# Another order for the guests of the last image: each chunk's score four places behind its variance

## The chip, the cores and the metric

The kernel runs on one core of a Trainium2 chip. The metric is device time in microseconds; smaller is better. The core's engines run side by side and are held together by semaphores alone: TensorE (PE) multiplies matrices and writes PSUM, VectorE (DVE) and ScalarE (ACT) compute element by element, GpSimd (POOL) multiplies the band of the attention and issues the stores of the output, SyncE (SP) issues the loads.

## What is computed

One layer of a vision transformer over a batch of four images. The patches of each image are embedded and a class token goes in front: 3137 tokens of 128 features. Then

```python
h = tok(x, tok_W, tok_b, tok_cls)
h = h + attn(layernorm(h), Wq, Wk, Wv, Wo, bias_table)      # 8 heads of 16
h = h + ffn(layernorm(h), attn_w, attn_b, gate_w, gate_b, w1, b1, w2, b2)

def ffn(x, ...):                       # x: the second layernorm's result
    aw = softmax(x @ attn_w + attn_b, axis=1)            # a score for each token
    pooled = sum(x * aw, axis=1)
    gates = softmax(pooled @ gate_w + gate_b)
    idx = top_k(gates, 2)                                # two of 8 experts per image
    g = gates * mask(idx); g = g / (sum(g) + 1e-9)
    h = gelu(x @ w1 + b1)                                # 128 -> 512
    eo = gelu(h @ w2 + b2)                               # 512 -> 128
    return sum over the two experts of eo * g
```

The gate of an image needs the scores of all its tokens, and these need the second layernorm of all its tokens.

## The kernel before

Features lie on the 128 partitions, tokens along the free dimension. An image has 8 chunks (`CH`) of W = 393 tokens. The kernel has three stages: embedding, first layernorm and projections; attention over 32 pairs of image and head; and the experts.

**Guests.** What lies between attention and experts is cut into 33 small pieces for each image, called guests, which stand as single steps inside another stage's stream. For a chunk c they are:

- Y: TensorE multiplies the chunk's attention output by Wo; VectorE adds it to `h_all` (line 1100).
- M: TensorE takes the mean over the features with the matrix `mean_w`; VectorE subtracts it (1104) and squares the difference into `sq2[c % 2]` (1106).
- V: TensorE takes the mean of the squares, the variance; VectorE adds epsilon into `root` (1108) and computes the reciprocal square root with `rstd`: a first guess from integer bits (1125), three Newton rounds of three instructions (1130, 1132, 1135 or 1137), and the multiplication of the chunk by the result (1140). That last instruction raises `s_ln2`.
- S: TensorE multiplies the normalized chunk by `pool_wr`; VectorE adds the bias (1112): the score.
- G, one for the image: the logits of the gate.

The guests of the first three images stand in the attention of the following image. Those of the last image have no attention left to stand in: they stand beside the steps of the expert loop.

**The expert loop.** 64 units (4 images, 8 chunks, 2 experts) and one step more. In step U TensorE does in this order: eight matmul instructions of the first layer of unit U (line 773), eight of the second layer of unit U - 1 (781), and, where `LATE` has a guest for the step, that guest (`visit`, 757). ScalarE does four Gelus of the hidden layer (916) and one of the output (923). VectorE accumulates the output of the unit before into `h_all` (1210) and then takes the guest's result out of PSUM (`receive`). Each engine works through its own list in order, and a wait holds back all that is behind it.

**The order.** `LATE` gives step 3 + i the guest number i of the last image, for i from 0 to 31; which guest that is comes from `guest_list`, the order of `guest_plan()`, which is laid out for the attention of the other images. Written out with the steps it begins Y0 3, M0 4, V0 5, S0 6, Y1 7, M1 8, Y2 9, V1 10, S1 11, M2 12, V2 13, S2 14, Y3 15, and ends Y7 31, M7 32, V7 33, S7 34. For each of the eight chunks S stands one step behind V. The maximum of the scores follows in step 36 (`pool_max`, VectorE), their exponential (`pool_exp`, ScalarE) in step 36 too, the pooling in 37, the gate guest in 39 and the choice of experts in 40.

**What a guest waits for** (`visit`, lines 735 to 757): Y for its chunk of attention output, which SyncE loads into `att[c % 4]`; M for its Y; V for the squares of its M (`s_sq2`); S for its chunk's normalization (`s_ln2`). All use the same PSUM bank (`LATE_PS`), so guest k also waits until k guests have been taken out by VectorE (`s_guest`). For V the first instruction (1108) counts as the taking, not the end of the chain.

**SyncE.** `load_attention(b, c)` (583 to 591) loads the chunks 0 to 3 of the last image at the end of the attention; the chunks 4 to 7 use the same four buffers and wait until Y of chunk c - 4 has been taken. `load_experts(b)` (593 to 602) loads the weights of two experts of an image. At the end of SyncE's list stand: the weights of the second image, the chunks 4 to 7, and the weights of the third and of the fourth image, each behind a step of the expert loop.

The lines that the change touches are the list of orders, `guest`, which turns a number into image, kind and chunk, and `guest_number`, which does the reverse.

Of the kernel before, what the change touches and what calls it, by code (L numbers as in the profile page):

```python
# [20 lines left out]
CH = 8  # L21
# [69 lines left out]
def guest_plan():  # L91

    seen = {"Y": 0, "M": 0, "V": 0, "S": 0}
    plan = []
    for p in range(1, 2 * HEADS):
        y_here = False
        for pos in GUEST_POS:
            if pos == GUEST_POS[2]:
                kinds = [("V", "M")]
            else:  # L100
                kinds = [("S", "V"), ("M", "Y"), ("Y", None)]
            for kind, after in kinds:
                c = seen[kind]
                if c < CH and (after is None or c < seen[after]) and not (kind == "Y" and y_here):
                    seen[kind] += 1
                    y_here = y_here or kind == "Y"
                    plan.append((kind, c, p, pos))
                    break
    assert len(plan) == 4 * CH and plan[-1][2] <= 13
    return plan + [("G", 0, 15, GUEST_POS[0])]  # L110


def fast_order(B, KT):

    NBH = B * HEADS
    PASS = 4 * KT
    units = [(n, kt, 4 * side + c) for n in range(NBH) for side in range(2) for kt in range(KT) for c in range(4)]
    plan = guest_plan()
    places = [(2 * HEADS * (b + 1) + p) * PASS + pos for b in range(B - 1) for kind, c, p, pos in plan]
    busy = {q // PASS for q in places} | {2 * HEADS * (b + 1) + p for b in range(B - 1) for p in (13, 14, 15)}  # L120
    wanted = [q * PASS + pos for q in range(1, 2 * NBH) for pos in ((33, 53) if q in busy else (28, 46, 64, 82))]

    def plain(u):

        n, kt, c = units[u]
        lo = kt * P - REACH
        return kt < KT - 1 and max(lo, c * (-(-((KT - 1) * P + 65) // CH)), 0) >= min(lo + BAND, (c + 1) * (-(-((KT - 1) * P + 65) // CH)))

    groups, guest_at, d_at, u = [], {}, {}, 0
    while u < len(units):  # L130
        size = GMAX
        if len(guest_at) < len(places) and u >= places[len(guest_at)]:
            guest_at[len(groups)] = len(guest_at)
            size = GMAX - 1
        elif len(d_at) < len(wanted) and u >= wanted[len(d_at)] and u + 2 < len(units) and plain(u + 2):
            d_at[len(groups)] = len(d_at)
        groups.append(list(range(u, min(u + size, len(units)))))
        u += size
    assert len(guest_at) == len(places)
    batches = [list(range(m, m + 4)) for m in range(0, len(units), 4)]  # L140
    return units, groups, batches, guest_at, d_at


def build(nc, B, S, d):
# [27 lines left out]
    with top:  # L172
# [34 lines left out]
        with ctx:  # L207
# [196 lines left out]
            GUESTS = 4 * CH + 1  # L404
            D_STEPS = 6
            EW = 16 * 8
            NU = 2 * CH
            GATE_OPS = 15
            guest_list = [(kind, c) for kind, c, p, pos in guest_plan()]
            chunk_pass = {c: p for kind, c, p, pos in guest_plan() if kind == "Y"}  # L410

            def guest(k):

                return (k // GUESTS,) + guest_list[k % GUESTS]

            def guest_number(b, kind, c):

                return b * GUESTS + guest_list.index((kind, c))

            def expert_unit(U):  # L420

# [73 lines left out]
            def _(sp):  # L495
# [87 lines left out]
                def load_attention(b, c):  # L583

                    if c >= 4:
                        sp.wait_ge(s_guest, guest_number(b, "Y", c - 4) + 1)
                    elif b > 0:
                        sp.wait_ge(s_guest, guest_number(b - 1, "Y", c + 4) + 1)
                    head = CH * 32 * W
                    src = bass.AP(att_rows, b * (HEADS * head) + c * 32 * W, [[head, HEADS], [W, HD], [1, W]])  # L590
                    sp.dma_start(att[:, c % 4], src).then_inc(s_att[c % 4], 16)
# [56 lines left out]
            def _(pe):  # L648
# [85 lines left out]
                def visit(k, bank):  # L734

                    b, kind, c = guest(k)
                    x = slice(c * W, (c + 1) * W)
                    if kind == "Y":
                        if k == 0:
                            pe.wait_ge(s_w3, 16 * 5)  # L740
                        pe.wait_ge(s_att[c % 4], 16 * (b * CH // 4 + c // 4 + 1))
                        weight, moving, n = wo[:], att[:, c % 4], W
                    elif kind == "M":
                        pe.wait_ge(s_guest, guest_number(b, "Y", c) + 1)
                        weight, moving, n = mean_w[:], h_all[:, b, x], W
                    elif kind == "V":
                        pe.wait_ge(s_sq2, b * CH + c + 1)
                        weight, moving, n = mean_w[:], sq2[:, c % 2], W
                    elif kind == "S":
                        pe.wait_ge(s_ln2, b * CH + c + 1)  # L750
                        weight, moving, n = pool_wr[:], x2[b][:, x], W
                    else:
                        pe.wait_ge(s_pooled, b + 1)
                        weight, moving, n = pooled[:], gate_w[:], E
                    if k > 0:
                        pe.wait_ge(s_guest, k)
                    nc.tensor.matmul(ps[:, bank, 0:n], weight, moving, start=True, stop=True).then_inc(s_guest_mm, 1)  # L757
# [231 lines left out]
            def _(dve):  # L989
# [103 lines left out]
                def receive(k, bank):  # L1093

                    b, kind, c = guest(k)
                    x = slice(c * W, (c + 1) * W)
                    came = ps[:, bank, 0:W]
                    dve.wait_ge(s_guest_mm, k + 1)
                    if kind == "Y":
                        nc.vector.tensor_tensor(h_all[:, b, x], h_all[:, b, x], came, ALU.add).then_inc(s_guest, 1)  # L1100
                    elif kind == "M":
                        if c == 0 and 0 < b < B - 1:
                            dve.wait_ge(s_ln2_out[b - 1], 16)
                        nc.vector.tensor_tensor(x2[b][:, x], h_all[:, b, x], came, ALU.subtract).then_inc(s_guest, 1)
                        dve.wait_ge(s_guest, k + 1)
                        nc.vector.tensor_tensor(sq2[:, c % 2], x2[b][:, x], x2[b][:, x], ALU.mult).then_inc(s_sq2, 1)
                    elif kind == "V":
                        nc.vector.tensor_scalar(root[:, 0], came, EPS, None, ALU.add).then_inc(s_guest, 1)
                        dve.wait_ge(s_guest, k + 1)
                        rstd(b, c, x)  # L1110
                    elif kind == "S":
                        nc.vector.tensor_scalar(sc2[b][:, x], came, pool_b[:, 0:1], None, ALU.add).then_inc(s_guest, 1)
                    else:
                        nc.vector.tensor_tensor(gt[:, b, 0], ps[:, bank, 0:E], gate_b[:], ALU.add).then_inc(s_guest, 1)
                        dve.wait_ge(s_guest, k + 1)
                        g0 = b * GATE_OPS
                        nc.vector.reduce_max(st[:, b, 5:6], gt[:, b, 0], AX_X).then_inc(s_gates, 1)
                        dve.wait_ge(s_gates, g0 + 1)
                        nc.vector.tensor_scalar(st[:, b, 6:7], st[:, b, 5:6], -1.0, None, ALU.mult).then_inc(s_lg, 1)
# [1017 lines left out]
```

## Time and profile before

| | |
|---|---|
| median of three runs | 2872.43 us (2869.24 to 2874.86) |
| the profiled execution | 2869.71 us, of which 2868.0 are the span |
| mean granted clock of TensorE | 0.986 |
| busy share of the span | TensorE 88%, ScalarE 88%, VectorE 56%, GpSimd 30% |
| attention | from 205 to 2453 us (first and last exponential of scores) |
| expert loop | from 2455 us to the end, the guests of the last image from 2474 us |

The span is the time from the first to the last instruction of the profiled execution. A timeline row gives the start in us from the span's start, the duration in us, the engine, the line of the kernel, the operation, what it writes and reads, the shape, and how many instructions are merged; in brackets stands the engine's idle time just before and what ended it. Names of tiles are those of the memory, which several tiles share: `halves` is `att`, `qk_sq` is `sq2`, `shared` is the normalized last image and its scores, `qa` and `ka` are the hidden layer and the output of the experts. A matmul's `x8` are four products of 128x128 by 128x393 in two instructions each; PEld is the loading of weights, which runs beside the matmuls.

### The profile page before, as it was taken

The page shows a single profiled execution, that of the slowest core. Times are in us where ns is not written, and L with a number is a line of the kernel's source. Part 1 is how long each engine was busy: PE and PEld are TensorE (multiplying, and loading weights), DVE is VectorE, ACT ScalarE, POOL GpSimd, SP SyncE. Part 2 cuts the span into 40 slices and gives each one's busy share as a digit, 9 for nine tenths or more (in the row PEclk, how much of TensorE's full clock was granted, in tenths as well). Part 3 has the DMA queues.
Part 4 walks back from the last instruction along what each step waited for, and adds up shares of the span by engine and source line. Part 5 has one row for each costly group of instructions (what it writes and reads, how often), then busy time and mean ns, then how long its engine had stood idle before and what let it go on. Part 6 is the DMA issues. An engine that isn't in the chain of part 4 may idle for free.

```text
span 2868.0 us, 123840 instructions
## 1 busy us (share of the span) xinstructions
PE 2534.1 (88%) x55860; PEld 1252.9 (44%) x55860; DVE 1616.4 (56%) x2542; ACT 2524.5 (88%) x2733; POOL 873.1 (30%) x1424
## 2 busy tenths in 40 slices
PE   7988888888888888988889898888989888999897
PEld 3444444444444444444444444444444444555454
DVE  5754777776756556555565565565655654443310
ACT  5669999999999999999999999999999999544453
POOL 2113443333333333333333333333333333100000
PEclk9989999999999999999999999999999999999999
DMA  5540101100101110011111000111110011210010
GB/s 145 172 163 12 38 32 33 32 29 29 41 29 35 32 32 29 29 51 43 30 36 33 29 29 29 51 40 35 32 32 29 29 52 46 91 35 14 14 35 19
DMA packets 65911, 125.43 MB, mean 44 GB/s; under 512 B 10034, under 2 KB 55180, under 8 KB 63892
## 3 DMA queue, kind: packets, MB, share of 16 engines
q1 hardware_dynamic: 63324, 110.93, 12.4%
q8 instruction: 446, 7.31, 1.1%
q0 software_dynamic: 2048, 6.43, 0.6%
q14 instruction: 93, 0.76, 0.1%
HBM read 67.30 MB, written 51.30 MB: 41 GB/s over the span
## 4 chain that ended last, share of the span: by engine, by line
ACT 46%; PE 25%; issue 18%; DVE 6%; DMA 3%; POOL 0%; SPq 0%; ACTq 0%; DVEq 0%; POOLq 0%
ACT shared L897 45%; PE ps L812 6%; PE ps L773 5%; PE ps L781 5%; PE ps L730 3%; PE ps L757 2%; PE ps L727 2%; DMA k_halves<-halves 1%; DVE root L1087 1%; PE ps L669 1%; DVE std L1019 1%; DVE root L1080 1%; DVE root L1078 1%; DVE root L1132 0%; DVE root L1130 0%
## 5 line engine op out<-in xcount | busy, mean ns | idle before, releaser
L897 ACT ACTIVATE shared<-ps 128x1179 f32<-128x1179 f32 (+1 forms) x2167 | 2205.8, 1181 | 34.1 <-PE ps L730 18.3
L812 PE MATMUL ps<-shared,va 64*32 64x393 f32 x25600 | 1565.4, 500 | 1.3 <-issue 0.9
L980 POOL TENSOR_TENSOR shared<-shared,e_all 128x310 f32<-128x310 f32 (+19 forms) x1344 | 814.9, 623 | 1441.5 <-ACT shared L897 1434.5
L730 PE MATMUL ps<-qa,ka 48*32 48x393 f16 (+1 forms) x15200 | 733.8, 319 | 138.3 <-ACT shared L897 122.2
L727 PE MATMUL ps<-qa,ka 51*32 51x393 f16 (+8 forms) x13184 | 658.9, 313 | 122.4 <-ACT shared L897 114.0
L812 PEld LDWEIGHTS ps<-shared,va 64*32 64x32 f32 x25600 | 617.3, 139 | 31.9 <-issue 5.2
L730 PEld LDWEIGHTS ps<-qa,ka 48*32 48x32 f16 x15200 | 242.6, 90 | 603.5 <-ACT shared L897 575.1
L727 PEld LDWEIGHTS ps<-qa,ka 51*32 51x32 f16 x13184 | 218.5, 89 | 641.4 <-ACT shared L897 621.8
L1057 DVE COPY xc<-ps 128x393 f32<-128x393 f32 x64 | 36.4, 569 | 533.2 <-PE ps L812 533.2
L1087 DVE SCALAR_TENSOR_TENSOR root<-root 128x393 f32<-128x393 f32 x486 | 319.6, 658 | 16.7
L916 ACT ACTIVATE qa<-ps,b 128x393 f32<-128x393 f32 x256 | 136.6, 586 | 111.6 <-PE ps L773 111.5
L1210 DVE SCALAR_TENSOR_TENSOR h_all<-ka,gsc,h_all 128x393 f32<-128x393 f32 x64 | 40.2, 628 | 263.5 <-ACT ka L923 263.5
L1078 DVE TENSOR_SCALAR root<-ps 128x393 f32<-128x393 f32 x162 | 91.8, 567 | 141.1 <-PE ps L727 71.3
L1065 DVE RECIPROCAL sq<-sq 128x393 f32<-128x393 f32 x64 | 167.4, 2615 | 2.2
L985 POOL DMA_DIRECT2D out<-h_all x32 | 18.0, 563 | 380.0 <-DVE h_all L1210 380.0
L923 ACT ACTIVATE ka<-ps,b 128x393 f32<-128x393 f32 x64 | 37.8, 591 | 98.3 <-PE ps L781 98.3
L1082 DVE SCALAR_TENSOR_TENSOR root<-root 128x393 f32<-128x393 f32 x162 | 109.5, 676 | 5.5
L1091 DVE SCALAR_TENSOR_TENSOR shared<-root 128x393 f32<-128x393 f32 x162 | 109.2, 674 | 5.5
L1019 DVE RECIPROCAL std<-std 128x393 f32<-128x393 f32 x32 | 83.7, 2615 | 34.0 <-ACT std L844 34.0
L1080 DVE SCALAR_TENSOR_TENSOR root<-root,ps 128x393 f32<-128x393 f32 x162 | 91.7, 566 | 5.5
L773 PE MATMUL ps<-shared,e_all 128*128 128x393 f32 x256 | 93.1, 508 | 0.0
L781 PE MATMUL ps<-qa,v_sb 128*128 128x393 f32 x256 | 89.9, 493 | 0.0
(149 smaller groups left out, 1629.7 us busy)
## 6 DMA issues: line engine op xcount, KB each, us to landing
qa<-q_halves SPq DMA_DIRECT2D x64, 196.5 KB
ka<-k_halves SPq DMA_DIRECT2D x64, 196.5 KB
att_rows<-std SPq DMA_DIRECT2D x64, 196.5 KB, 4.0
v_rows<-v_sb SPq DMA_DIRECT2D x4, 1600.0 KB, 6.9
va<-v_rows SPq DMA_DIRECT2D x32, 200.0 KB, 15.9
ln_rows<-ln SPq DMA_DIRECT2D x32, 196.5 KB, 5.6
q_halves<-halves SPq DMA_DIRECT2D x32, 196.5 KB, 3.1
k_halves<-halves SPq DMA_DIRECT2D x32, 196.5 KB, 4.3
```

Source lines behind the costliest of these rows:

```text
L727: last = nc.tensor.matmul(out[x:y, 0:cut], ka[r:r + 51, par, k0 + x:k0 + y], qa[r:r + 51, par, q0:q0 + cut], start=True, stop=True, tile_p ...
L730: last = nc.tensor.matmul(out[x:y, cut:W], ka[r:r + 48, par, k0 + x:k0 + y], qa[r:r + 48, par, q0 + cut:q0 + W], start=True, stop=True, ti ...
L773: last = nc.tensor.matmul(ps[:, HID_PS + sl, 0:W], w1[b % 2][:, e, sl * P:(sl + 1) * P], ln2[b][:, c * W:(c + 1) * W], start=True, stop=True)
L781: last = nc.tensor.matmul(ps[:, EO_PS + U % 2, 0:W], w2[b % 2][:, e, sl], hid[:, (U - 1) % 2, sl], start=(sl == 0), stop=(sl == HS - 1))
L812: last = nc.tensor.matmul(ps[quad:quad + 32, O_PS + half, 0:W], va[r:r + 64, par, :, kt], pr[r:r + 64, g % SLOTS_PR, j], start=(kt == 0), ...
L897: nc.scalar.activation(pr[:, g % SLOTS_PR, 0:m], ps[:, b0:b0 + m, 0:W], ACT.Exp, scale=-1.0 / (LOG2E * LIFT * LIFT)).then_inc(s_exp, 1)
L916: last = nc.scalar.activation(hid[:, U % 2, sl], ps[:, HID_PS + sl, 0:W], ACT.Gelu, bias=b1[:, 2 * (b % 2) + e, sl:sl + 1])
L980: nc.gpsimd.tensor_tensor(p, p, e_all[0:keys, n % HEADS, t:t + z - a], ALU.mult).then_inc(s_biased, 1)
L1065: nc.vector.reciprocal(inv[:, side], inv[:, side]).then_inc(s_inv, 1)
L1078: nc.vector.tensor_scalar(whole, score, EXP2_OFFSET, ROUND, ALU.add, ALU.add).then_inc(s_d_step, 1)
L1080: nc.vector.scalar_tensor_tensor(x, whole, ROUND, score, ALU.subtract, ALU.subtract).then_inc(s_d_read, 1)
L1087: nc.vector.scalar_tensor_tensor(p, p, EXP2[3 - i], x, ALU.add, ALU.mult).then_inc(s_d_step, 1)
```

## The change

A function `late_order` builds another order for the 33 guests of the last image. It walks over CH + 3 rounds; in round s stand the transform of chunk s, the mean of chunk s - 1, the variance of s - 2 and the score of s - 3, each where there is such a chunk, and G at the end. `guest` and `guest_number` use it for the last image and the old list for the others. The steps of the loop at which guests stand, and the engines' code for each kind, are the same. The unused `chunk_pass` goes.

```diff
+def late_order():
+
+    steps = []
+    for s in range(CH + 3):
+        for kind, lag in (("Y", 0), ("M", 1), ("V", 2), ("S", 3)):
+            if 0 <= s - lag < CH:
+                steps.append((kind, s - lag))
+    return steps + [("G", 0)]
...
             guest_list = [(kind, c) for kind, c, p, pos in guest_plan()]
-            chunk_pass = {c: p for kind, c, p, pos in guest_plan() if kind == "Y"}
+
+            late_list = late_order()
 
             def guest(k):
 
-                return (k // GUESTS,) + guest_list[k % GUESTS]
+                return (k // GUESTS,) + (guest_list if k // GUESTS < B - 1 else late_list)[k % GUESTS]
 
             def guest_number(b, kind, c):
 
-                return b * GUESTS + guest_list.index((kind, c))
+                return b * GUESTS + (guest_list if b < B - 1 else late_list).index((kind, c))
```

The new order is Y0, Y1, M0, Y2, M1, V0, Y3, M2, V1, S0, Y4, M3, V2, S1, and so on in fours, with Y7, M6, V5, S4, M7, V6, S5, V7, S6, S7 at the end.

## Rows read from the trace of the kernel before

**Rows 1.** The page: the span; busy us, share and instructions of each engine.

```profile
span 2868.0 us, 123840 instructions
...
PE 2534.1 (88%) x55860; PEld 1252.9 (44%) x55860; DVE 1616.4 (56%) x2542; ACT 2524.5 (88%) x2733; POOL 873.1 (30%) x1424
```

**Rows 2.** Waits of TensorE from 2453 us on: us in total, times, longest.

```profile
PE ps L757 <- DVE shared L1140: 18.5, 8, 2.4
PE ps L773 <- ACT qa L916: 5.0, 1, 5.0
```

**Rows 3.** Timeline of TensorE: Y0, V0, S0 [idle before it], Y1.

```profile
2473.93 0.82 PE L757 MATMUL ps<-halves,wo 128*128 128x393 f32 x2
...
2485.82 0.82 PE L757 MATMUL ps<-qk_sq,mean_w 128*128 128x393 f32 x2
...
2494.23 0.93 PE L757 MATMUL ps<-shared,pool_wr 128*128 128x393 f32 x2 [2.30 <-DVE shared L1140]
...
2500.28 0.82 PE L757 MATMUL ps<-halves,wo 128*128 128x393 f32 x2
```

**Rows 4.** Timeline of TensorE: V1, S1, the group behind, the next guest.

```profile
2518.12 0.82 PE L757 MATMUL ps<-qk_sq,mean_w 128*128 128x393 f32 x2
...
2526.54 1.00 PE L757 MATMUL ps<-shared,pool_wr 128*128 128x393 f32 x2 [2.31 <-DVE shared L1140]
2527.33 4.47 PE L773 MATMUL ps<-ln,v_sb 128*128 128x393 f32 x8
...
2534.28 0.82 PE L757 MATMUL ps<-h_all,mean_w 128*128 128x393 f32 x2
```

**Rows 5.** Timeline of ScalarE in one step of the expert loop.

```profile
2506.43 0.59 ACT L923 ACTIVATE ka<-ps,b 128x393 f32<-128x393 f32 x1 [1.58 <-PE ps L781]
2508.47 1.07 ACT L916 ACTIVATE qa<-ps,b 128x393 f32<-128x393 f32 x2 [1.45 <-PE ps L773]
2509.73 1.07 ACT L916 ACTIVATE qa<-ps,b 128x393 f32<-128x393 f32 x2 [0.19 <-PE ps L773]
```

**Rows 6.** Timeline of VectorE: accumulation, V0 taken, its chain's end, accumulation.

```profile
2486.64 0.63 DVE L1210 SCALAR_TENSOR_TENSOR h_all<-ka,gsc,h_all 128x393 f32<-128x393 f32 x1 [4.24 <-ACT ka L923]
2487.19 0.56 DVE L1108 TENSOR_SCALAR root<-ps 128x393 f32<-128x393 f32 x1
...
2493.61 0.57 DVE L1140 SCALAR_TENSOR_TENSOR shared<-root,shared 128x393 f32<-128x393 f32 x1
2494.09 0.62 DVE L1210 SCALAR_TENSOR_TENSOR h_all<-ka,gsc,h_all 128x393 f32<-128x393 f32 x1
```

**Rows 7.** Windows behind S0, S1: busy us by engine, clock, DMA share, GB/s.

```profile
2494.20:2502.20 8.00, 7.97 (x24) 4.66 (x25) 2.23 (x4) 2.73 (x5) 0.54 (x1) 1.00 0.07 25
2526.50:2534.50 8.00, 7.96 (x19) 4.49 (x20) 1.15 (x2) 2.15 (x5) 0.00 (x0) 0.79 0.00 0
```

**Rows 8.** Timeline of TensorE: the group 32 steps behind the first guest.

```profile
2691.61 2.80 PE L773 MATMUL ps<-shared,v_sb 128*128 128x393 f32 x8
```

**Rows 9.** Timeline of SyncE's queue: loads of attention chunks and ln rows.

```profile
2462.74 2.72 SPq L591 DMA_DIRECT2D halves<-att_rows  x4
2465.56 0.94 SPq L607 DMA_DIRECT2D shared<-ln_rows  x2
...
2478.01 1.10 SPq L591 DMA_DIRECT2D halves<-att_rows  x1
```

**Rows 10.** Windows while the loads run, columns as in group 7.

```profile
2470.00:2480.00 10.00, 10.00 (x32) 5.77 (x31) 1.20 (x3) 4.86 (x9) 0.71 (x1) 1.00 1.03 379
2480.00:2484.00 4.00, 4.00 (x14) 2.31 (x13) 1.67 (x3) 2.29 (x5) 0.55 (x1) 1.00 0.59 181
```

**Rows 11.** Timeline of TensorE: the group behind the wait on ScalarE.

```profile
2707.33 5.00 PE L773 MATMUL ps<-shared,v_sb 128*128 128x393 f32 x8 [4.99 <-ACT qa L916]
```

**Rows 12.** Windows without a stall, columns as in group 7.

```profile
2455.20:2491.80 36.60, 36.60 (x114) 20.62 (x110) 13.91 (x23) 17.92 (x33) 1.26 (x2) 1.00 0.49 162
2712.20:2844.70 132.50, 132.50 (x404) 76.22 (x403) 19.73 (x47) 70.94 (x129) 7.05 (x13) 1.00 0.08 27
```

## The prediction

> **What bounds the kernel now.** I read the page first: TensorE and ScalarE are each busy for 88% of the span [rows 1], an average over three different stages, so it prices nothing. The change reaches only the guests of the last image, the small matmuls that stand between the steps of the expert loop, from about 2474 us on. So I asked second what TensorE waited for from the loop's start to the end of the kernel: 18.5 us in eight waits on line 1140, the last instruction of the normalization on VectorE, and one of 5.0 us on ScalarE; there is nothing else [rows 2]. The timeline of TensorE shows the form. A step of the loop with a guest takes 5.95 us: from 2500.28 to 2518.12 there are three of them, 17.84 us, so 5.947 each [rows 3, 4]. Its matmuls stand back to back, thus TensorE sets the pace, and ScalarE idles 1.58 + 1.45 + 0.19 = 3.2 us in each [rows 5]. The exception is the score guest S, which stands one place behind the variance guest V of the same chunk: V0 at 2485.82, S0 not one step later, at 2491.77, but at 2494.23, after 2.30 us idle [rows 3].
>
> VectorE shows why. V's matmul starts at 2485.82; the accumulation of the step goes first (2486.64), line 1108 takes V's result at 2487.19, and the chain ends with line 1140, at 2493.61 + 0.57 = 2494.18 [rows 6], 8.36 us behind V. S reads what that line writes, and TensorE works in order, so all expert matmuls behind S stand still.
>
> The granted clock adds a second loss. Behind S0 the clock stays at 1.00; behind S1 the same 2.31 us of idle time is followed by a stretch at 0.79, in which eight matmuls take 4.47 us rather than 2.80 [rows 4, 7]: part of it at the lower of TensorE's two levels (1.2 against 2.4 GHz). Of the eight stalls, those of chunks 0, 2, 4 and 6 look like the first, those of 1, 3, 5 and 7 like the second: windows of 8 us behind each show 1.00 four times and 0.79 four times, of which one of either kind stands there.
>
> **What a stall costs.** Measured from the start of V to the start of the guest behind S, two steps, which need 2 x 5.947 = 11.89 us. Short kind: 2500.28 - 2485.82 = 14.46, so 2.57 us. Long kind: 2534.28 - 2518.12 = 16.16, so 4.27 us, 1.70 of them the clock's. Four of each: 4 x (2.57 + 4.27) = 27.4 us. A second way that doesn't need the pairs: from the first guest (2473.93) to the start of the group that stands 32 steps behind it (2691.61, [rows 8]) are 217.68 us; 32 steps of 5.947 are 190.3; the difference is 27.4 us.
>
> **What the change does.** It removes no instruction and adds none: the same 32 guests stand at the same steps, 3 to 34, and only their order differs; the maximum, the exponential, the pooling and the gate guest stay at steps 36 to 40. Written out, the variances now stand at steps 8, 11, 15, 19, 23, 27, 30 and 32, and the scores at 12, 16, 20, 24, 28, 31, 33 and 34. So the distance is 4, 5, 5, 5, 5, 4, 3 and 2 steps: four only at the start, and two for the last chunk. Two suffice: S7's turn comes 11.89 us behind V7, and the chain is through after 8.36, with 3.5 us in hand. All eight stalls go, with the clock falls behind them: gain 27.4 us.
>
> **What is late next.** Each guest also waits until the guest before it has been taken out of the one PSUM bank. Now something other than its own score stands behind every variance. That guest is taken only when VectorE is through with the chain, and the guest after it waits for that. From the rows: the chain is through at +8.36, the accumulation at 2494.09 + 0.62 = +8.89, taking a result costs some 0.56 more, as at line 1108 [rows 6], so about +9.5; the matmul that needs the bank has its turn at +11.89. Slack 2.4 us: no stall, price 0, and if the slack weren't there, each us over it would cost 8 us in all. The other distances (transform Y to mean M at least 2, M to V at least 3) are longer than or equal to those of before, where no such pair stalled. VectorE's work per guest is unchanged. ScalarE's wait for an accumulation reaches back more than one step, and the accumulation that the chain delays ends at +8.89 in the old order as well; ScalarE keeps its 3.2 us of idle time. Price 0.
>
> **The moved loads.** The transforms Y1, Y2 and Y3 move from steps 7, 9 and 15 to 4, 6 and 9, and their chunks of the attention output are among the four that SyncE issued from 2462.74 on, ahead of two loads of ln rows at 2465.56 [rows 9] and of the experts' weights. Y1 is the tight one: it now has the turn of 2479.87, 5.95 us behind the first guest. From 2470 to 2480 the DMA engines are full, and by 2484 the queue is nearly empty [rows 10]. The chunks were issued first, some 15 us ahead, and Y0's chunk, of the same group, was there at 2473.93 without a wait; I take price 0. The other end: the chunk comes as the last of all, at 2484, which costs 4.1 us and, with a clock fall, 5.8, and leaves 21.6 us of the gain. The Trainium skill ("DMA: Bandwidth & Descriptors", section "Two DMAs through the same engine are not ordered") says that nothing orders transfers across the 16 DMA engines, so being issued first promises nothing about landing first; by that rule the gain could be 21.6 us in place of 27.4. No row here gives the landing of these chunks.
> The loads of chunks 4 to 7 wait on SyncE for Y0 to Y3. The first was issued at 2478.01 [rows 9], when SyncE was through with the weights, and is needed at step 13, that is at 2473.93 + 10 x 5.947 = 2533; the others are asked for at steps 4, 6 and 9 and needed at 17, 21 and 25, at least 13 steps or 77 us later. Queued behind them on SyncE are the weights of the third image, which wait for a step (17) that doesn't move in the order; they are needed at step 32. Price 0.
>
> **What stays.** The 5.0 us wait on ScalarE behind the last score [rows 2], with matmuls of 5.00 instead of 2.80 us behind it [rows 11], lies at a fixed step and comes 27 us earlier. Its clock fall costs 2.2 us and could come out somewhat larger or smaller: plus or minus 2 us.
>
> **Sum.** The profiled execution took 2869.7 us, a span of 2868.0 and 1.7 around it; less 27.4 this is 2842.3. It lies 2.7 us under the median of the three runs, 2872.43. The forecast is for a median: 2872.4 - 27.4 = **2845.0 us**.
>
> **The rivals.**
> - *The clock falls stay.* If the half-rate stretches have another cause than the stalls, 4 x 1.70 = 6.8 us remain: 2851.8. For it: four equal stalls had none, so the stall alone doesn't decide. Against it: outside of stalls the clock is at 1.00 over 36.6 and over 132.5 us of unbroken matmuls [rows 12]. Chance 4%.
> - *Y1's chunk is late*: 2872.4 - 21.6 = 2850.8. Chance 3%.
> - *Two or three steps are not enough for the last chunks*: if VectorE began the chains of V6 and V7 late, S6 and S7 would stall as now, 2.57 + 4.27: 2851.8. Against it the 3.5 us of slack. Chance 3%.
> - *The change doesn't do what it says.* A wait of the same length takes the stall's place, at the second guest behind each V, because the bank is taken later than I derive: 2872.4. Against it the 2.4 us of slack, eight times in the same form. Chance 3%.
> - *Slower.* The pauses are what keeps TensorE at its upper level, and 190 us without any bring it down for part of the time. Each us of work at 1.2 GHz costs one more. Up to 27.4 of the 190.3 us (14%) at the lower level the kernel still gains, beyond that it loses; with 20% it is 2845.0 + 38 = 2883. Against it stand the 132.5 us at 1.00 at the end of this very loop [rows 12]. Chance 2%.
>
> **How the numbers follow.** The forecast has 85%. A measurement of this kernel can tell about 0.2%, 5.7 us, from no change; the forecast is 1.0% down, and the first three rivals 0.7%. So faster 95%, same 3%, slower 2%. The range: the three runs of before spread over 2869.2 to 2874.9, 3 us to each side, and the term at the ScalarE wait adds 2: 2840 to 2850. It leaves out all rivals, 15%, of which two begin just above it.
>
> **What would show it.** In the profile after: no wait of TensorE on line 1140 in the loop; 32 steps of 5.95 us between the first guest and the group behind the last, 190 us rather than 218; the granted clock at 1.00 over them; a score's matmul starting right behind the expert matmuls while VectorE has been through for several us; the ScalarE wait of 5 us as before; no wait of TensorE before the second Y. I would be wrong if idle time appears on TensorE two steps behind a variance, if matmuls of 4.4 us per eight stand without a stall ahead of them, or if the stretches before 2474 us differ by more than a few us from one run to the next.

## The result and the profile after

The changed kernel takes 2843.11 us (median of four runs, 2842.16 to 2845.30) against 2871.71 us beside it (2869.24 to 2874.86): a ratio of 0.9901, 95% interval 0.9884 to 0.9918, so 28.6 us or 1.0% faster. The forecast was 2845.0 in a range of 2840 to 2850. The profiled execution took 2842.38 us with a span of 2840.7; against the 2869.71 and 2868.0 of before that is 27.3 us.

Lines behind the new function have moved by 11: line 757 is now 768, 773 is 784, 781 is 792, 916 is 927, 1108 is 1119, 1140 is 1151, 1210 is 1221.

The page's busy line of after, which answers to the one in [rows 1]: the same number of instructions on each engine, and TensorE's busy time 12.7 us shorter, though nothing was taken out. Of these, 8.8 us lie in the guests' stretch (199.12 against 190.30 in the two windows below); 6.8 of them are the matmuls that ran at the lower clock, as an experiment below shows.

```profile
PE 2521.4 (89%) x55860; PEld 1249.2 (44%) x55860; DVE 1614.3 (57%) x2542; ACT 2523.4 (89%) x2733; POOL 872.5 (31%) x1424
```

The waits of TensorE from 2453 us on, which answer to [rows 2] (what waited, for what: us in total, times, longest). The eight waits on the end of the chain are not there; the one on ScalarE is, unchanged.

```profile
PE ps L784 <- ACT qa L927: 5.0, 1, 5.0
```

The timeline of TensorE in the loop, which answers to [rows 3, 8, 11]: Y0, Y1, V0, the guest behind it (Y3), the one behind that (M2), S0, the group 32 steps behind the first guest, and the group behind the wait on ScalarE.

```profile
2473.40 0.82 PE L768 MATMUL ps<-halves,wo 128*128 128x393 f32 x2
...
2479.35 0.82 PE L768 MATMUL ps<-halves,wo 128*128 128x393 f32 x2
...
2503.14 0.82 PE L768 MATMUL ps<-qk_sq,mean_w 128*128 128x393 f32 x2
...
2509.08 0.82 PE L768 MATMUL ps<-halves,wo 128*128 128x393 f32 x2
...
2515.03 0.82 PE L768 MATMUL ps<-h_all,mean_w 128*128 128x393 f32 x2
...
2526.92 0.82 PE L768 MATMUL ps<-shared,pool_wr 128*128 128x393 f32 x2
...
2663.69 2.80 PE L784 MATMUL ps<-shared,v_sb 128*128 128x393 f32 x8
...
2679.41 5.15 PE L784 MATMUL ps<-shared,v_sb 128*128 128x393 f32 x8 [4.99 <-ACT qa L927]
```

No guest has idle time ahead of it. From the first guest to the group behind the last are 2663.69 - 2473.40 = 190.29 us, 5.947 a step; before it was 217.68. S0 starts 23.8 us behind V0, when its chain has been through for 15.

VectorE over the same variance, which answers to [rows 6]: accumulation, V0 taken, the end of the chain, the next accumulation, and the guest behind V (Y3) taken.

```profile
2503.96 0.63 DVE L1221 SCALAR_TENSOR_TENSOR h_all<-ka,gsc,h_all 128x393 f32<-128x393 f32 x1 [4.24 <-ACT ka L934]
2504.50 0.56 DVE L1119 TENSOR_SCALAR root<-ps 128x393 f32<-128x393 f32 x1
...
2510.93 0.57 DVE L1151 SCALAR_TENSOR_TENSOR shared<-root,shared 128x393 f32<-128x393 f32 x1
2511.42 0.62 DVE L1221 SCALAR_TENSOR_TENSOR h_all<-ka,gsc,h_all 128x393 f32<-128x393 f32 x1
2511.95 0.56 DVE L1111 TENSOR_TENSOR h_all<-h_all,ps 128x393 f32<-128x393 f32 x1
```

The chain is as long as before, through 8.36 us behind V (2510.93 + 0.57 - 2503.14). The guest behind V is taken by 2511.95 + 0.56 = 2512.51, and the matmul that needs its bank has its turn at 2515.03: 2.5 us in hand.

The guests' 32 steps as one window in the trace of before and in that of after (columns as in group 7; the clock is the third number from the end):

```profile
2474.00:2691.60 217.60, 199.12 (x577) 111.60 (x576) 88.80 (x160) 87.31 (x160) 9.16 (x16) 0.97 0.11 36
```

```profile
2473.40:2663.70 190.30, 190.30 (x578) 109.23 (x577) 88.08 (x160) 87.15 (x160) 9.14 (x16) 1.00 0.12 40
```

TensorE idled 18.5 us of the 217.6 and is now busy without a gap; VectorE and ScalarE did the same work in both.

### The profile page after: what moved, and what is told of

Same layout as the page of the kernel before. It is cut to its first block, busy times and chain, and to the rows that moved or that the text cites. A ratio compares the mean times of both kernels' runs of the same rounds, so it can differ in the third digit from the quotient of the medians.

```text
span 2840.7 us, 123840 instructions
## 1 busy us (share of the span) xinstructions
PE 2521.4 (89%) x55860; PEld 1249.2 (44%) x55860; DVE 1614.3 (57%) x2542; ACT 2523.4 (89%) x2733; POOL 872.5 (31%) x1424
## 4 chain that ended last, share of the span: by engine, by line
ACT 47%; PE 27%; issue 18%; DVE 4%; DMA 3%; SPq 0%; POOL 0%; ACTq 0%; DVEq 0%; POOLq 0%
ACT shared L908 46%; PE ps L784 6%; PE ps L792 6%; PE ps L823 6%; PE ps L741 3%; PE ps L768 3%; PE ps L738 2%; DMA k_halves<-halves 2%; DVE root L1098 1%; DVE std L1030 1%; DVE root L1091 1%; DVE root L1089 1%; PE ps L680 1%; PE ps L674 0%; PE ps L695 0%
## 5 line engine op out<-in xcount | busy, mean ns | idle before, releaser
L741 PE MATMUL ps<-qa,ka 48*32 48x393 f16 (+2 forms) x15200 | 732.9, 319 | 139.4 <-ACT shared L908 122.9
L792 PE MATMUL ps<-qa,e_all 128*128 128x393 f32 x256 | 89.7, 493 | 0.0
```

The costliest lines, as they stand in the source:

```text
L741: last = nc.tensor.matmul(out[x:y, cut:W], ka[r:r + 48, par, k0 + x:k0 + y], qa[r:r + 48, par, q0 + cut:q0 + W], start=True, stop=True, ti ...
L792: last = nc.tensor.matmul(ps[:, EO_PS + U % 2, 0:W], w2[b % 2][:, e, sl], hid[:, (U - 1) % 2, sl], start=(sl == 0), stop=(sl == HS - 1))
```

## The experiments

The theory: TensorE waited, in order, for the chain of the same chunk; that cost 2.30 us of idle time eight times, and part of these pauses brought a fall of the clock. The rivals: that the distances of Y, M and V or the earlier loads brought something; that four places are needed; that the clock falls have another cause; that a wait behind the variance is close by.

All kernels were profiled. The third column is the stretch from the first guest to the group behind the last, read as above, which holds every step that the change touches; the last is its mean granted clock.

| kernel | median us (of before beside it) | 32 steps, us | clock |
|---|---|---|---|
| before | 2871.71 | 217.68 | 0.97 |
| after | 2843.11 (2871.71) | 190.29 | 1.00 |
| score directly behind its variance | 2872.97 (2872.54) | 217.54 | 0.97 |
| old order, score one place later | 2846.37 (2872.54) | 192.91 | 1.00 |
| old order, two rounds | 2852.61 (2872.54) | 196.43 | 1.00 |
| old order, four rounds | 2899.87 (2871.22) | 241.40 | 0.92 |
| old order, pauses filled | 2864.46 (2872.54) | 210.88 | 1.00 |
| new order, four rounds | 2847.46 (2871.22) | 190.29 | 1.00 |
| new order, five rounds | 2854.78 (2871.22) | 200.77 | 1.00 |

### The new order with each score directly behind its variance

```diff
-        for kind, lag in (("Y", 0), ("M", 1), ("V", 2), ("S", 3)):
+        for kind, lag in (("Y", 0), ("M", 1), ("V", 2), ("S", 2)):
```

Expected: 

> The new order with one thing undone: the score of chunk s - 2 is placed in the same round as its variance, so that every S again stands one step behind its own V, while Y, M and V stay apart as in the changed kernel. Theory (S directly behind V is all that the old order cost): the eight waits on the last instruction of the chain come back with 2.3 us each, a step pair of 14.5 us without and 16.2 us with a clock fall, so the time is that of after, 2843.1, plus 8 x 2.57 = 20.6 and 1.7 for each fall: 2863.7 with none, 2870.5 with four, 2877 with eight. Rival (the earlier loads, or the distances of Y, M and V, brought the gain): 2843 to 2850 and no such waits. How often the clock falls is open; the theory says only that it falls behind stalls.

Measured: 2872.97 us, ratio 1.0003 (0.9988 to 1.0018), 2.5 us above what was expected with four clock falls: all of the gain is gone. The waits of TensorE and its timeline at V2, S2, the group behind and the next guest:

```profile
PE ps L768 <- DVE shared L1151: 18.5, 8, 2.4
```

```profile
2567.33 0.82 PE L768 MATMUL ps<-qk_sq,mean_w 128*128 128x393 f32 x2
...
2575.74 1.17 PE L768 MATMUL ps<-shared,pool_wr 128*128 128x393 f32 x2 [2.30 <-DVE shared L1151]
2576.70 4.30 PE L784 MATMUL ps<-shared,e_all 128*128 128x393 f32 x8
...
2583.48 0.82 PE L768 MATMUL ps<-halves,wo 128*128 128x393 f32 x2
```

The same eight waits with the same 18.5 us as in [rows 2], and again the clock fell behind four of the eight: 2583.48 - 2567.33 = 16.15 us is the long kind. They are other ones than before: windows of 8 us behind each show 0.79 or 0.80 for chunks 2, 3, 5 and 7. Y, M and V follow one another as in the changed kernel, from Y3 on one step later because S0 stands ahead of it, and Y1 and Y2 need their chunks as early. The stretch is that of before to 0.14 us. So the distance between V and S is the whole effect, and the other moves bring and cost nothing.

### The old order with the scores one place later

```diff
+    steps = [(kind, c) for kind, c, p, pos in guest_plan()]
+    for c in range(CH - 1):
+        i = steps.index(("S", c))
+        steps[i], steps[i + 1] = steps[i + 1], steps[i]
```

(This stands in `late_order` in place of the four rounds, so it acts on the last image alone; `steps` starts as the old list.)

Expected: 

> The old order with the smallest step away from it: the scores of chunks 0 to 6 change places with the guest behind them, so they stand two steps behind their variance; the last chunk's score stays one behind. Theory (two places are enough, since the chain is through 8.4 us behind V and the turn of S comes at 11.9): seven of eight stalls go, one of 2.57 or 4.27 us stays, 2871.7 - 27.4 + 2.6 to 4.3 = 2846.9 to 2848.6, and the only wait of TensorE on the chain is at the last score. Rival (four places are what it takes): stalls remain at all scores, the time is above 2855.

Measured: 2846.37 us, ratio 0.9912 (0.9889 to 0.9935), half a us below the expected 2846.9 to 2848.6. TensorE's wait on the chain, and its timeline at V0 and S0:

```profile
PE ps L767 <- DVE shared L1150: 2.4, 1, 2.4
```

```profile
2484.21 0.82 PE L767 MATMUL ps<-qk_sq,mean_w 128*128 128x393 f32 x2
...
2496.10 0.82 PE L767 MATMUL ps<-shared,pool_wr 128*128 128x393 f32 x2
```

S0 starts 11.89 us behind V0 without idle time; the one wait on the chain that is left is that of the last chunk, whose score wasn't moved, and it is of the short kind: 192.91 - 190.29 = 2.62 us. For the seven scores that were moved, two places do all that the new order does.

### The old order with a shorter and with a longer chain

```diff
-                    r0 = (b * CH + c) * 9
+                    rounds = 3 if b < B - 1 else 2
+                    r0 = (b * CH + c) * 9 if b < B - 1 else b * CH * 9 + c * 3 * rounds
...
-                    for i in range(3):
+                    for i in range(rounds):
...
-                        if i < 2:
+                        if i < rounds - 1:
```

(The other kernel has 4 in place of the 2. With two rounds the root is less exact; that kernel leaves work out.)

Expected with two rounds: 

> The old order with two rounds of the root iteration in place of three for the last image: three instructions of VectorE fewer in each chain (the root is less exact; that part of the work is left out), 3 x 0.603 = 1.81 us. Theory (TensorE waits for the length of this chain): each stall shrinks from 2.30 to 0.5 us of idle time, 8 x 1.81 = 14.5 us go, and with them the clock falls (6.8) as the pauses are too short for one: 2871.7 - 14.5 - 6.8 = 2850.4. If the falls stay for all their shorter pauses: 2857.2. Rival (the wait has another cause, such as the bank): 2871.7.

Expected with four: 

> The old order with a fourth round of the root iteration for the last image: three instructions of VectorE more in each chain, 1.81 us. Theory: the idle time ahead of each score grows from 2.30 to 4.1 us, 8 x 1.81 = 14.5 us, 2887 with as many clock falls as before; with a fall behind each of the eight longer pauses up to 4 x 1.7 = 6.8 more, 2894. Rival (the chain is hidden elsewhere): 2872.5.

Measured with two: 2852.61 us, ratio 0.9930 (0.9904 to 0.9957). TensorE at V1, S1, the group behind, the next guest:

```profile
2522.05 0.82 PE L757 MATMUL ps<-qk_sq,mean_w 128*128 128x393 f32 x2
...
2528.65 0.93 PE L757 MATMUL ps<-shared,pool_wr 128*128 128x393 f32 x2 [0.49 <-DVE shared L1141]
2529.41 2.80 PE L773 MATMUL ps<-ln,v_sb 128*128 128x393 f32 x8
...
2534.70 0.82 PE L757 MATMUL ps<-h_all,mean_w 128*128 128x393 f32 x2
```

Idle time 2.31 became 0.49: the 1.81 us of three instructions, one for one. The group behind takes 2.80 us, and no fall is left in the stretch: 217.68 - 196.43 = 21.25 us, where 14.5 + 6.8 = 21.3 was expected. (The median lies 2.2 us above the expected 2850.4; this excess is not in the stretch, see the last section.)

Measured with four: 2899.87 us, ratio 1.0090 (1.0068 to 1.0112). Here the expectation (2887 to 2894) missed. The same places:

```profile
PE ps L757 <- DVE shared L1141: 32.9, 8, 4.2
```

```profile
2530.15 0.82 PE L757 MATMUL ps<-qk_sq,mean_w 128*128 128x393 f32 x2
...
2540.37 1.68 PE L757 MATMUL ps<-shared,pool_wr 128*128 128x393 f32 x2 [4.11 <-DVE shared L1141]
2541.84 5.02 PE L773 MATMUL ps<-ln,v_sb 128*128 128x393 f32 x8
...
2549.34 0.82 PE L757 MATMUL ps<-h_all,mean_w 128*128 128x393 f32 x2
```

The wait grew by 1.81 us as expected (32.9 - 18.5 = 14.4). What was mis-sized is the clock. All eight pauses are followed by slow matmuls, and some of the falls cost more than the 1.7 us that was assumed for each. Two steps without a loss take 11.89 us, the pause adds 4.11 and, as with the short kind of before, 0.27 more: 16.27. The pairs took 17.8 to 19.2, here 2549.34 - 2530.15 = 19.19, so 1.5 to 2.9 us of clock loss for each, 16.1 in all against 6.8 in the old order. The stretch is thus 241.40 - 217.68 = 23.7 us longer. The median is 28.6 above that of before beside it; in the profiled execution the loop also began later (first guest at 2482.46), of which more below.

### The pauses filled with matmuls that nobody reads

```diff
                     elif kind == "S":
+                        if b == B - 1:
+                            for _ in range(3):
+                                nc.tensor.matmul(ps[:, LATE_PS + 1, 0:W], mean_w[:], ln[:, 0:W], start=True, stop=True)
                         pe.wait_ge(s_ln2, b * CH + c + 1)
```

Expected: 

> The old order, and ahead of each score's wait TensorE computes three products of 128x128 by 128x393 whose result nobody reads, 6 instructions of 0.33 us, 1.98 us, in what was idle time. The wait itself stays, and its end is set by VectorE as before. Theory (the clock falls come from the pauses): with 0.3 us of idle time left in place of 2.3 there is no fall, the four stretches at 0.79 go to 1.00, 4 x 1.70 = 6.8 us: 2864.9, and every pair of steps takes 14.5 us. Rival (the falls have another cause, or the pauses matter only as time): four falls stay and it is 2871.7 as before.

Measured: 2864.46 us, ratio 0.9971 (0.9958 to 0.9984), 8 us faster than before with 48 matmul instructions more. TensorE at V1, the filler, S1, the group behind, the next guest:

```profile
2525.11 0.82 PE L760 MATMUL ps<-qk_sq,mean_w 128*128 128x393 f32 x2
...
2531.06 2.14 PE L752 MATMUL ps<-ln,mean_w 128*128 128x393 f32 x6
2533.52 0.93 PE L760 MATMUL ps<-shared,pool_wr 128*128 128x393 f32 x2 [0.32 <-DVE shared L1143]
2534.29 2.80 PE L776 MATMUL ps<-ln,v_sb 128*128 128x393 f32 x8
...
2539.57 0.82 PE L760 MATMUL ps<-h_all,mean_w 128*128 128x393 f32 x2
```

S1 starts 8.41 us behind V1, as in [rows 4] (2526.54 - 2518.12 = 8.42): the wait is untouched. But the pair takes 14.46 us rather than 16.16, and so do all the others; the stretch is 217.68 - 210.88 = 6.80 us shorter, to the digit the clock's share. That splits the 27.4 us of the change into 20.6 of waiting (210.88 - 190.29) and 6.8 of clock, and shows that without the pauses there are no falls. It doesn't show what decides which of the equal pauses brings one.

### The new order with a longer chain

The same edit as above, with four and with five rounds for the last image in the new order.

Expected with four: 

> The new order with the same fourth round: the chain is through at 8.36 + 1.81 = 10.2 us behind V, the next guest is taken at about 11.3, and the guest after it has its turn at 11.89. Theory (a slack of 2.4 us in the new order): 0.6 us are left, TensorE doesn't wait, 2843 as without the round. Rival (the slack is smaller than worked out, the bank's release comes later): a wait of TensorE on VectorE's taking of the guest appears two steps behind each V, 8 x up to 1 us, 2851.

Expected with five: 

> The new order with a fourth and a fifth round, 3.62 us more in each chain. Theory: the slack of 2.4 us is overrun by 1.2; the next guest is taken at about 13.1 us behind V, so the guest after it starts 1.2 to 1.4 us late, eight times, 10 to 11 us: 2853 to 2854, and some clock falls of up to 1.7 us could come on top, up to 2862. The wait stands on the instruction that takes the guest behind V, not on the end of the chain. Rival (with the scores far away the chain doesn't reach TensorE at all): 2843.

Measured with four: 2847.46 us (2842.38 to 2856.17), ratio 0.9921 (0.9897 to 0.9945). VectorE at the end of the chain of V0 (whose matmul started at 2509.10), and TensorE at the second guest behind it:

```profile
2518.70 0.57 DVE L1152 SCALAR_TENSOR_TENSOR shared<-root,shared 128x393 f32<-128x393 f32 x1
...
2519.72 0.56 DVE L1111 TENSOR_TENSOR h_all<-h_all,ps 128x393 f32<-128x393 f32 x1
```

```profile
2520.99 0.82 PE L768 MATMUL ps<-h_all,mean_w 128*128 128x393 f32 x2
```

The guest behind V is taken by 2520.28, 0.7 us ahead of the next one's turn. The stretch takes 190.29 us, as without the round: 14.5 us more work on VectorE cost nothing. In the old order the same round cost 23.7. The median lies 4 us over the expected 2843, but the excess is not in this stretch.

Measured with five: 2854.78 us, ratio 0.9947 (0.9927 to 0.9967). TensorE's waits on VectorE, and its timeline at the guest behind V0, the second behind V0, and the next:

```profile
PE ps L768 <- DVE shared L1123: 7.5, 7, 1.1
...
PE ps L768 <- DVE h_all L1111: 1.1, 1, 1.1
```

```profile
2512.13 0.82 PE L768 MATMUL ps<-halves,wo 128*128 128x393 f32 x2
...
2519.31 0.90 PE L768 MATMUL ps<-h_all,mean_w 128*128 128x393 f32 x2 [1.08 <-DVE h_all L1111]
...
2525.33 0.82 PE L768 MATMUL ps<-qk_sq,mean_w 128*128 128x393 f32 x2
```

The wait that was to come next is there, eight times, at the place that the prediction named: two steps behind each variance, on the instruction that takes the guest between (L1111 for a Y, L1123 for a score). 200.77 - 190.29 = 10.5 us, expected 10 to 11, and the clock didn't fall behind pauses of 1.1 us.

### Where the loads land

That Y1's chunk comes late was a rival that no row could settle. In the trace of after TensorE doesn't wait for it; how much time is in hand shows when the guests are moved up. This kernel puts all guests two steps earlier:

```diff
-            LATE = {3 + i: (B - 1) * GUESTS + i for i in range(4 * CH)}
+            LATE = {1 + i: (B - 1) * GUESTS + i for i in range(4 * CH)}
```

Expected: 

> The new order with all 32 guests two steps earlier, from step 1 on, to see when the chunks of the attention output land that the second transform needs early. Y0's turn comes at about 2463, right behind the issue of its chunk, Y1's one step later, 5.3 us before any row so far bounds its landing. Theory (the chunks issued first also land first): TensorE waits some 3 to 5 us at Y0 and not at Y1, so chunk 1 is there by about 2473, 7 us ahead of its turn in the changed kernel; the whole costs those 3 to 5 us. Rival (the chunks land among the ln rows and weights, at 2477 to 2484): TensorE waits at Y1 again for 4 us or more.

Measured in a single execution: 2851.27 us. SyncE's issue of the four chunks, here and in the changed kernel:

```profile
2468.53 2.72 SPq L602 DMA_DIRECT2D halves<-att_rows  x4
```

```profile
2462.41 2.72 SPq L602 DMA_DIRECT2D halves<-att_rows  x4
```

TensorE at Y0 and Y1, with the guests moved up:

```profile
2472.35 0.90 PE L768 MATMUL ps<-halves,wo 128*128 128x393 f32 x2 [3.16 <-issue]
...
2478.37 0.82 PE L768 MATMUL ps<-halves,wo 128*128 128x393 f32 x2
```

TensorE waits 3.2 us at Y0 and not at all at Y1. The profile names nothing that ended the wait (`issue`), but the code lets Y0 wait for its chunk, which is then there 3.8 us behind the first issue. So Y1's chunk has landed within 9.8 us of the first issue. In the changed kernel Y1's turn comes 16.9 us behind it (2479.35 - 2462.41): at least 7 us in hand. The rival is out. The Trainium skill ("DMA: Bandwidth & Descriptors", "Two DMAs through the same engine are not ordered") is not contradicted by this: it promises no order, and here what was issued first was there in time.

The pause cost about its length, a little less than the 3 to 5 us expected: from the loop's first matmul to the end of the span it is 2849.6 - 2460.83 = 388.8 us, and 2840.7 - 2454.63 = 386.1 in the changed kernel, 2.7 more; this has 0.6 us less for the matmuls behind the wait on ScalarE, which took 4.54 us in place of 5.15. Behind this pause of 3.16 us the clock didn't fall: it is 1.00 over the whole 190.36 us up to the group 32 steps on. The rest of the 8 us lies ahead of the loop.

### The maximum of the scores one step earlier

The pause of 5.0 us that stays comes from two things in a row: VectorE's maximum (line 1155), for which ScalarE waits 2.9 us, and ScalarE's exponential of the scores (893), which stands between two loads of a function table. In the changed kernel:

```profile
2669.78 1.28 ACT L893 ACT_TABLE_LOAD   x1
...
2670.34 3.42 DVE L1155 TENSOR_REDUCE st<-shared 128x1 f32<-128x3137 f32 x1
...
2673.98 2.91 ACT L893 ACTIVATE shared<-shared,st 128x3137 f32<-128x3137 f32 x1 [2.92 <-DVE st L1157]
...
2677.00 1.28 ACT L927 ACT_TABLE_LOAD   x1
```

The new order leaves nothing to wait for in step 35, so the maximum can stand there.

```diff
-            LATE_MAX, LATE_EXP, LATE_POOL, LATE_GATE, LATE_GEXP, LATE_PICK = 36, 36, 37, 39, 39, 40
+            LATE_MAX, LATE_EXP, LATE_POOL, LATE_GATE, LATE_GEXP, LATE_PICK = 35, 36, 37, 39, 39, 40
...
                     if U == LATE_MAX:
+                        dve.wait_ge(s_guest, B * GUESTS - 1)
                         pool_max(B - 1)
```

Expected: 

> The new order, and the maximum of the scores stands one step earlier, 35 in place of 36, behind a wait for the last score. The exponential on ScalarE stays in step 36. Before, ScalarE waited 2.9 us for this maximum, and TensorE 5.0 us for ScalarE. Theory: the maximum is through before ScalarE comes to it, 2.9 us go from that one wait, leaving 2.1, and the clock fall behind it (2.2 us) can go as well: 2843.1 - 2.9 = 2840.2, down to 2838. Rival (ScalarE's two table loads and the exponential are what TensorE waits for): 5.0 us as before, 2843.

Expected in a second comparison: 

> The new order with the maximum of the scores at step 35, against the changed kernel on the same chip. In the first look the stretch from the first guest to the end took 363.2 us against 367.3. Theory: the 4 us hold in the whole time, so the median lies 4 us (0.15%) below that of the changed kernel beside it. Rival (the time ahead of the loop varies by more than that and hides it): no difference of the medians can be told, though the stretch is shorter again.

And of the changed kernel beside it: 

> The changed kernel once more, for a comparison on the same chip with the version whose maximum stands a step earlier: 2843 to 2845, 367.3 us from the first guest to the end. All theories agree on it; it gives the scatter of what lies before the loop.

Measured first: 2844.81 us (2836.80 to 2848.66), not the 2838 to 2840.2 that was expected. In the second comparison, on one chip: 2840.69 (2837.12 to 2843.77) against 2843.77 (2842.43 to 2849.45) for the changed kernel; against before, 0.9889 (0.9871 to 0.9906) and 0.9905 (0.9889 to 0.9921). From the second comparison, TensorE's wait:

```profile
2682.45 2.91 PE L784 MATMUL ps<-shared,v_sb 128*128 128x393 f32 x8 [2.09 <-ACT qa L927]
```

and the same place in the first:

```profile
2686.86 4.60 PE L784 MATMUL ps<-shared,v_sb 128*128 128x393 f32 x8 [2.09 <-ACT qa L927]
```

4.99 us became 2.09, by the 2.9 expected, in both. The clock fall went in one and stayed in the other. From the first guest to the end of the span: 363.2 and 362.2 us, against 367.3 and 367.1 for the changed kernel. The stretch is 4 to 5 us shorter. In the whole time the median is 3.1 us below that of the changed kernel beside it, where 4 was expected, and the intervals overlap. That this version is faster is shown for the stretch and not for the whole time.

## Why the prediction was right

- **What TensorE waits for.** Chain of the same chunk, in order: shown by undoing the distance alone (217.54 against 217.68 us) and by the response to the chain's length, 1.81 us for 1.81.
- **The price of a stall**, 2.57 and 4.27 us: the sum said 27.4, the stretch gave 217.68 - 190.29 = 27.39. The profile of before held this number, since the step of 5.947 us was a clean measure of what is left when the wait goes.
- **Two steps are enough**: shown in the old order. The four places of the title, in truth two to five as the prediction lists them, aren't what matters.
- **The clock's share** of 6.8 us: shown by filling the pauses. The step that was weakest in the argument, as four equal stalls had no fall, was right. Why a fall follows one pause and not its equal stays open.
- **What is late next**: slack worked out at 2.4, read in after at 2.5; one more round (1.81) fits, two (3.62) don't, and the wait comes up where it was named.
- **The loads** at price 0: right, with 7 us in hand or more. The prediction had taken this without a row for the landing. (That the queue was nearly empty by 2484 isn't in [rows 10] either, which end there at a share of 0.59.)
- **The wait on ScalarE stays**: 4.99 us in both. From the group behind the last guest to the end of the span it was 2868.0 - 2691.61 = 176.39 before and 2840.7 - 2663.69 = 177.01 after; the 0.6 lies in the term of plus or minus 2.
- **The slower rival**, a clock that falls under unbroken work: 190.3 us at 1.00 without a gap, so it is out.
- **The range** was narrower than it should have been in one term. It took the scatter from three runs (2869.2 to 2874.9). The kernel before gave 2863.7 to 2879.3 in the comparisons since. The medians held; a single execution of after could have left 2840 to 2850.
- **Where luck helped**: the 2845.0 and the 2843.11 differ by 1.9 us, 0.7 of it because before measured 2871.71 in place of 2872.4. Against a scatter of several us ahead of the loop, so close a hit of the whole time is in part luck; the 27.39 us of the stretch isn't.

## What to carry to other kernels

Where engines work in order and pieces of a chain are dealt out to the steps of a loop, compare the time from a piece's start to the end of what the next needs with the loop's step: here 8.36 against 5.95 us, so one place is too few and two are enough. Measure a stall over the whole pair of steps, not by the idle time: 2.30 us of idle time cost 2.57 or 4.27. And once a chain is off the path, work out whom its engine serves next; that wait had 2.5 us in hand and would otherwise have been the new bound.

## What was not expected

**A pause is paid for unevenly.** Pauses of the same 2.30 us were followed by slow matmuls in four of eight cases in the old order, each time at 1.7 us, and in four other cases of eight with the score directly behind. Those of 0.3, 0.5 and 1.1 us in the kernels above never were, those of 4.11 in all eight cases, at 1.5 to 2.9 us, and that of 2.09 in one execution of two. Length alone doesn't decide: the pause of 3.16 us ahead of Y0 (guests two steps earlier) had no fall behind it. So to lengthen a wait by 1.81 us cost 23.7 us over eight, not 14.5, and to shorten it gave 21.3.

**The time ahead of the loop varies by more than many a change.** All kernels here have the same instructions up to it, and yet its first matmul started between 2453.6 (scores one place later) and 2466.1 us (score directly behind). A good part is there before the attention. The first 206 us of before and of the kernel with filled pauses (columns as in group 7):

```profile
0.00:206.00 206.00, 173.67 (x614) 87.55 (x614) 134.00 (x120) 126.83 (x225) 40.20 (x48) 0.97 0.55 162
```

```profile
0.00:206.00 206.00, 176.72 (x570) 89.17 (x571) 130.77 (x107) 120.68 (x218) 40.15 (x48) 0.91 0.52 154
```

In the same time TensorE is through with 614 matmuls in one and 570 in the other, at a mean clock of 0.97 and 0.91, and the first exponential of the attention starts at 205.2 and at 213.0 us. Why the clock differs there wasn't tried. For a change in one stage the stretch of that stage tells 0.1 us where the whole time tells 5.
